# A two-layer MetaFormer with top-2 experts on one Trainium2 core: the second expert bias copied into PSUM, the first experts' weights split earlier, and less work on GpSimd ahead of the routing

## The reference, cut to what matters

```python
x = x + _L0_conv_ref(_ln_c(x), W_qkv, W_proj, b_proj)        # attention over 24 positions, 16 heads
t = _to_tokens(x)
t = t + _L0_ffn_ref(_ln_t(t), gate_w, gate_b, w1, b1, w2, b2)
# layer 0, F = 1024
    for i in range(8):
        h = silu(xf @ w1[i] + b1[i])
        y = h @ w2[i] + b2[i]
        out = out + y * comb[:, i:i + 1]
# layer 1, I = 672
    for e in range(8):
        a, g = split(x @ W1[e] + b1[e], 2)
        out = out + cw[:, e:e + 1] * ((a * silu(g)) @ W2[e] + b2[e])
```

## Time and profile before

| what | value |
|---|---|
| median of three runs | 651.71 us (649.32 to 656.35) |
| the profiled execution's own time | 656.72 us |
| its span, first to last instruction | 655.0 us |
| PE busy | 583.5 us, 89% of the span |
| ACT, DVE, POOL busy | 330.0, 321.6, 291.9 us |
| bias matmuls, line 1342 | 56 |
| layer 0: attention and norms, routing, block loop | about 0 to 80, 80 to 110, 110 to 325 us |
| layer 1: the same | about 325 to 402, 402 to 433, 433 to 655 us |

### The profile page before, as it was taken

How to read it: one execution, slowest core, us unless ns; L and a number is a source line. 1 busy time by engine, 2 the same in 40 slices (tenths; PEclk the granted TensorE clock), 3 DMA queues, 4 the chain that set the end, 5 groups by cost and what they waited for, 6 DMA issues and landing times.

```text
span 655.0 us, 15545 instructions
## 1 busy us (share of the span) xinstructions
PE 583.5 (89%) x3702; PEld 505.7 (77%) x3703; DVE 321.6 (49%) x721; ACT 330.0 (50%) x586; POOL 291.9 (45%) x305
## 2 busy tenths in 40 slices
PE   8997966999999999998879877789999898999982
PEld 4976724888889888987559764279989898999982
DVE  6547583344442445443175386734545454666430
ACT  5683303556554666663157723135656464656430
POOL 3785213355444445544236641324545353555332
PEclk9999678999999999998779987779999898999987
DMA  7425754145432442325122248342254545222120
GB/s 233 132 71 173 241 198 153 25 135 136 125 65 37 125 104 64 69 42 149 21 83 87 85 149 266 131 135 34 38 156 114 160 109 131 74 66 41 36 31 11
DMA packets 43625, 69.35 MB, mean 106 GB/s; under 512 B 5280, under 2 KB 35024, under 8 KB 43600
## 3 DMA queue, kind: packets, MB, share of 16 engines
q1 hardware_dynamic: 32656, 54.86, 26.4%
q0 software_dynamic: 10944, 14.17, 12.1%
HBM read 56.43 MB, written 13.63 MB: 107 GB/s over the span
## 4 chain that ended last, share of the span: by engine, by line
PE 64%; DVE 12%; DMA 12%; issue 5%; ACT 2%; DVEq 2%; ACTq 1%; POOL 1%; POOLq 0%
PE banks L1125 14%; PE banks L1127 13%; PE banks L1126 13%; DMA out_dram<-expert_io,scol 6%; PE banks L1333 5%; PE banks L1156 4%; DMA mid_dram<-expert_io,scol 4%; PE banks L1133 2%; PE banks L1217 2%; DVE stats L830 2%; PE banks L1251 2%; PE banks L1302 2%; DVE onehot_row L1013 2%; PE banks L1240 1%; DVE raw L849 1%
## 5 line engine op out<-in xcount | busy, mean ns | idle before, releaser
L1125 PE MATMUL banks<-w_hi,hT_hi 128*128 (+1 forms) x392 | 120.1, 306 | 14.3 <-DVE hT_lo L1095 14.2
L1125 PE MATMUL banks<-w_hi,xT_hi 128*128 x336 | 121.7, 362 | 3.3 <-DVE xT_lo L1053 2.6
L1127 PE MATMUL banks<-w_hi,xT_lo 128*128 x336 | 116.3, 346 | 0.0
L1126 PE MATMUL banks<-w_lo,xT_hi 128*128 x336 | 115.8, 345 | 0.0
L1127 PE MATMUL banks<-w_hi,hT_lo 128*128 (+1 forms) x392 | 115.2, 294 | 0.0
L1126 PE MATMUL banks<-w_lo,hT_hi 128*128 (+1 forms) x392 | 115.1, 294 | 0.0
L1125 PEld LDWEIGHTS banks<-w_hi,hT_hi 128*128 128x128 f32 (+1 forms) x392 | 78.9, 201 | 21.4 <-issue 20.9
L768 ACT COPY banks<-seed_rows 128x1024 f32 (+1 forms) x58 | 66.7, 1151 | 39.3 <-issue 13.5
L1113 DVE TENSOR_SCALAR expert_io<-banks,gate_tab 128x256 f32<-128x256 f32 x56 | 27.1, 484 | 115.0 <-PE banks L1127 55.3
L599 POOL DMA_INDIRECT mid_dram<-expert_io,scol x28 | 57.6, 2057 | 56.4 <-DVE expert_io L1113 56.4
L561 POOL TENSOR_TENSOR w_lo<-raw,w_hi 128x1024 fp32r<-128x1024 f32 (+1 forms) x24 | 57.2, 2400 | 52.1 <-ACT w_hi L641 51.9
(11 more groups left out here) (188 smaller groups left out, 963.5 us busy)
## 6 DMA issues: line engine op xcount, KB each, us to landing
raw<-in_L_ffn_w_dram SPq DMA_DIRECT2D x32, 512.0 KB, 4.1
raw<-in_L_ffn_W_dram SPq DMA_DIRECT2D x16, 672.0 KB, 4.9
raw<-in_L_ffn_W_dram SPq DMA_DIRECT2D x16, 336.0 KB, 6.1
seed_rows<-in_L_ffn_b_dram SPq DMA_DIRECT2D x8, 672.0 KB, 4.6
seed_rows<-in_L_ffn_b_dram SPq DMA_DIRECT2D x8, 512.0 KB, 4.2
xn_dram<-raw SPq DMA_DIRECT2D x6, 512.0 KB, 3.0
xres<-in_x_dram SPq DMA_DIRECT2D x3, 512.0 KB, 4.5
wqkv<-in_L_conv_W_qkv_dram SPq DMA_DIRECT2D x2, 768.0 KB, 5.9
```

The source lines that it names most:

```text
L1125: pe.matmul(out, hi, w_high, start=first, stop=False, skip_group_check=onto)
L1126: pe.matmul(out, hi, w_low, start=False, stop=False, skip_group_check=onto)
L1127: return pe.matmul(out, lo, w_high, start=False, stop=last, skip_group_check=onto)
```

## The change

1. The bias matmul 1342 goes, and with it `bias_rows`, `expert_sel`, their DMAs, casts, subtractions and selects. SP loads the expert's b2 row, broadcast to 128 partitions, behind its b1 row (two DMAs per expert). ACT copies it to bank 6 in a new `seed_y(b)` at the very end of its `step(b)`, after the weight casts. `seed_y(b)` waits until DVE has read y of block b-1 (`e_sb`), for block 0 until an added fifth `swept` matmul (on bank 6, between PE's step 0 and step 1). PE's second product waits for `y_seeded`. ACT loads two experts from the table in each step instead of one.
2. The first experts' parts are loaded without SP waiting for each; ACT waits for a semaphore of the part (`part_in`). In layer 1 pieces 0 and 1 are cast before the first norm. Piece 3 moves ahead of the exponentials, 4 and 5 into the attention, 8 and 9 take the places between the copies of the product with the values, 10 and 11 come before the square roots of the second norm.
3. POOL makes its second set of constants at the start of the program, and no longer adds `bproj`: DVE does, after the softmax and before its copies of the product with the values.

```diff
             def load_seed(L, e):
-                sp.dma_start(seed_row(L, e % SLOTS), ffn_w[L][3][e].partition_broadcast(P)).then_inc(seed_dma, 16)
+                row, wide = seed_row(L, e % SLOTS), FFN[L].wide
+                sp.dma_start(row[:, 0:wide], ffn_w[L][3][e].partition_broadcast(P)).then_inc(seed_dma, 16)
+                sp.dma_start(row[:, wide:wide + C], ffn_w[L][5][e].partition_broadcast(P)).then_inc(seed_dma, 16)
...
+                    if e < SLOTS:
+                        sp.dma_start(to, src).then_inc(part_in[part], 16)
+                    else:
+                        sp.dma_start(to, src).then_inc(raw_dma[half], 16)
+                        loads[half] += 1
...
-                    if e < SLOTS:
-                        sp.wait_ge(raw_dma[half], 16 * loads[half])
...
-                        act.wait_ge(s.first_in, q + 1)
+                        act.wait_ge(part_in[q % PIECES], 16 * (SLOTS * L + q // PIECES + 1))
...
+                if L == 1:
+                    act.wait_ge(lay[0].moe_done, 1)
+                    first_high(0, 2)
...
                 first_high(2, 3)
                 values_out(2)
+                first_high(3, 4)
                 exponentials(0)
                 exponentials(1)
                 values_out(3)
-                first_high(3, 4)
+                first_high(4, 5)
...
                 attn_out(1)
+                first_high(5, 6)
                 values_out(6)
...
-                first_high(PIECES, PIECES + 2)
+                first_high(6, 8)
...
-                        first_high(PIECES + 2 + j // 2, PIECES + 3 + j // 2)
+                        first_high(8 + j // 2, 9 + j // 2)
...
-                nc.scalar.copy(bias_rows[:, :], bias_raw[:, :]).then_inc(s.bias_cast, 1)
+                first_high(10, 12)
                 nc.scalar.activation(table_out[0:BN, 2 * L:2 * L + 1], row_sum[:, 0:1], ACT.Sqrt)
-                first_high(2 * PIECES, 2 * PIECES + 1)
                 deviations(s.var2, 0, s.std2)
-                first_high(2 * PIECES + 1, 2 * PIECES + 2)
                 deviations(s.var2, 1, s.std2)
-                first_high(2 * PIECES + 2, 2 * PIECES + 3)
...
+                def seed_y(b, e):
+                    if after(b, 1):
+                        act.wait_ge(s.e_sb, b)
+                    else:
+                        act.wait_ge(swept, 5 * (L + 1))
+                    nc.scalar.copy(bank[6][:, 0:C], seed_row(L, e % SLOTS)[:, f.wide:f.wide + C]
+                                   ).then_inc(s.y_seeded, 1)
...
-                    e_next = expert_of(b + 1)
+                    e_here, e_next = expert_of(b), expert_of(b + 1)
                     pieces = piece_range(act, b)
                     xT_high(b + 1)
                     seed(b + 1, e_next)
                     for_pieces(act, pieces, lambda q: split(q, b))
+                    seed_y(b, e_here)
...
+                for g in range(3):
+                    tiles = slice(4 * g, 4 * g + 4)
+                    nc.vector.tensor_tensor(xres[:, tiles, :], xres[:, tiles, :],
+                                            bproj[:, :].unsqueeze(1).to_broadcast([P, 4, C]), ALU.add).then_inc(s.b_added, 1)
                 for j in range(1, 8, 2):
                     dve.wait_ge(s.av_mm, j + 1)
...
-                    if after(b, 1):
-                        pe.wait_ge(s.e_sb, b)
-                    pe.matmul(bank[6][:, 0:C], expert_sel[:, e, :], bias_rows[:, :],
-                              start=True, stop=False)
+                    pe.wait_ge(s.y_seeded, b + 1)
```

More of the change, by code:

```diff
@@ L286, in metaformer @@
         seed_in = sem("seed_in")
+        part_in = [sem(f"part_in{i}") for i in range(PIECES)]
         raw_dma = [sem(f"raw_dma{i}") for i in range(2)]
@@ L409, in load_expert @@
                 kt2 = f.kt // 2
-                for to, src, end in ((w1[:, 0, :], src1[:, 0, :], f.wide), (w1[:, 1, :], src1[:, 1, :], KC * f.wide),
-                                     (w2[:, 0:kt2, :], src2[:, 0:kt2, :], KC * f.wide + kt2 * C),
-                                     (w2[:, kt2:, :], src2[:, kt2:, :], WORDS[L])):
+                parts = ((w1[:, 0, :], src1[:, 0, :], f.wide), (w1[:, 1, :], src1[:, 1, :], KC * f.wide),
+                         (w2[:, 0:kt2, :], src2[:, 0:kt2, :], KC * f.wide + kt2 * C),
+                         (w2[:, kt2:, :], src2[:, kt2:, :], WORDS[L]))
+                for part, (to, src, end) in enumerate(parts):
                     pieces = -(-end // (WORDS[L] // PIECES))
@@ L419, in load_expert @@
                         sp.wait_ge(lay[L].pool_split, PIECES * (e - 1) + pieces)
-                    sp.dma_start(to, src).then_inc(raw_dma[half], 16)
-                    loads[half] += 1
+                    if e < SLOTS:
[3 more added lines that the diff above has]
+                        loads[half] += 1
                     if e >= SLOTS + 2 and pieces == -(-f.wide // (WORDS[L] // PIECES)):
                         seed_loaded(L, e - 2)
-                    if e < SLOTS:
-                        sp.wait_ge(raw_dma[half], 16 * loads[half])
-                        there = end // (WORDS[L] // PIECES)
-                        for _ in range(there - handed[0]):
-                            sp.sem_inc(lay[L].first_in, 1)
-                        handed[0] = there % PIECES
             def expert_loaded(L, half):
@@ L517, in _ @@
             pool.sem_inc(const_done, 1)
+            made(pool.memset(after_or_at[:, :], -1.0))
+            made(pool.affine_select(out=after_or_at[:, :], in_=after_or_at[:, :], compare_op=ALU.is_ge, fill=0.0,
+                                    base=0, pattern=[[-1, P]], channel_multiplier=1))
+            made(pool.memset(ones[:, :], 1.0))
+            made(pool.iota(iota_i[:, :], pattern=[[1, P]], base=0, channel_multiplier=0))
+            made(pool.tensor_copy(iota[:, :], iota_i[:, :]))
@@ L519, in _ @@
+            made(pool.memset(gather_tab[:, TAB:TABLE], 0))
+            made(pool.memset(scan_keep[:, :, :], 1.0))
+            made(pool.memset(scan_keep[:, :, 0:1], 0.0))
+            pool.sem_inc(const_done, 1)
             for L in range(2):
                 s = lay[L]
[L522 to L527 removed]
@@ L747, in _ @@
                 nc.scalar.activation(small[:, 0, :], small[:, 0, :], ACT.Exp).then_inc(s.exp8, 1)
-                act.wait_ge(s.bias_sub, 2)
-                nc.scalar.copy(bias_rows[64:96, :], bias_raw[64:96, :]).then_inc(s.bias_cast, 1)
                 act.wait_ge(s.tab, 2)
@@ L1374, in _ @@
                 pe.wait_ge(s.tab, 3)
+                pe.matmul(bank[6][:, 0:C], busy_in[:, :],
+                          busy_in[:, :].unsqueeze(1).to_broadcast([P, C // P, P]), start=True, stop=True
+                          ).then_inc(swept, 1)
                 step(1)
```

92 lines of the change are left out of this document (21 added, 71 removed).

## The result

The kernel after takes 673.63 us (median of four runs, 669.34 to 674.79), the kernel before beside it 650.78; the ratio on record is 1.0328 (1.0257 to 1.0400); the quotient of the two medians is 1.035. The forecast was 649.3 in a range of 640 to 659. The profiled executions span 671.0 and 655.0 us, 16 apart. The medians are 22.9 apart: the profiled execution of the kernel before was the longest of its four, so the traces show less loss than the medians.

A forecast was written before the change was run, and what follows sets the result against it. PE was taken to bound the kernel, with 64% of the chain. Terms of -11.2 us ahead of the loops, +3.2 for first blocks and +5.6 for the loops gave -2.4, from 651.7 to 649.3 us, range 640 to 659.

The forecast's parts named there:

- b2 broadcasts cost nothing that the chain shows: Loads of the second bias, broadcast to 128 partitions: no cost was counted for them.
- The ring: Block loops: ACT's copy waits for DVE's output, which waits for ACT; 7.1 us per block in layer 0, both loops +5.6.
- longer ring: Rival: ACT's queue from new copy to `xT_hi` takes 0.35 us more per block, loops +15.5, kernel 659.2; chance 0.17.
- Layer 1: Its block loop: 6.8 us per block, PE's pace, but double weight casts and lost catching up after late scatters: +3.8 us.
- The first block: Block 0 of each layer: PE's second product resumes 1.75 us late in layer 0, 1.5 in layer 1; together +3.2.
- The second norm: Ahead of the loops: POOL no longer collides with DVE's normalisation, PE's clock stays up; 6.0 us saved per layer.
- Between the loops: Layer 1 ahead of its loop: norm -6.0, routing -1.6, waits for pieces 8 and 9 +2.4, first block +1.5 us.
- DVE's moved additions: Three `bproj` additions on DVE, about 1.24 us each, 3.7 in a gap of 6.07: no cost.
- the rival of the pieces: Second norm: last pieces stay in the way, one collision and the low clock remain per layer; +4.8, 656.5 us; chance 0.1.
- the port rule: DVE and POOL contend for one port pair, the later blocks fully; three blocked additions cost up to 2.5 us per layer: 654.

The follow-up runs named there:

- after_late: The kernel after with only the second bias's broadcast moved behind the expert's last weight part, with its own semaphore: 661.55 us, 1.0177.
- p23_b2: Parts 2 and 3 on the kernel before, bias matmul kept, plus second-bias broadcasts for experts 3 to 7 into an unread row: 656.96 us, 1.0080.
- p23: The kernel before with parts 2 and 3 of the change alone, bias matmul kept: 645.42 us, 0.9899.
- late89: `p23` with layer 1's splits of pieces 8 and 9 put behind the copies, with 10 and 11: 647.47 us, 0.9951.
- p1: The kernel before with part 1 alone, ACT's copy of the b2 row in place of the bias matmul: 680.9 us, 1.0459.
- moved: The kernel after with the b2 copy taken from the end of ACT's step to behind the next step's `hT_hi` casts: 657.88 us, 1.0089.
- b2late: `moved` with the second bias's broadcast issued whole behind the expert's last weight part, with its own semaphore: 646.43 us, 0.9933.

## Why the prediction was wrong

- **The step that failed outright** is the half sentence that the "b2 broadcasts cost nothing that the chain shows". They cost 12.1 us in the kernel after (25.4 less the 13.3 of `after_late`), 10.6 where the matmul is kept, mostly by making scatters at an expert's change longer: `p23_b2` against `p23`, six of them by 1.0 to 1.6 us. The chain of before already gave DMA 12%, and the late scatters stood there; I had priced the added loads against the queue's mean load and not against the transfer that they fly beside. No rival of the prediction held it. Of the page of the Trainium skill "DMA: Bandwidth & Descriptors", the section "Queues, rings and completion order" says that each DMA engine goes round between the queue rows it has work for and drains a whole packet of one before it turns to the next. Its direction agrees: a load on SyncE's row delays a scatter on GpSimd's. No run shows the packets themselves.
- **The ring was right in kind and mis-sized**: 13.3 us by the loops, 15 to 16 by the medians (below), instead of 5.6. In layer 0 it cost 6.8 instead of 1.8. Round it by the rows above: `xT_hi` start to output end 2.54 in the rows of the chain (forecast 2.53); end of the output 189.17 to the copy 0.18 (0.1); copy to `hT_hi` 0.49 (0.27); `hT_hi` to `xT_hi` 4.01 (4.16). 7.2 instead of 7.06, with most blocks at 7.3. The 0.49 was not thought of: the copy ends the step, so the loop's own branch lies between it and the next instruction. In the chain of the kernel after:

```profile
189.35 0.05 ACT banks L732
189.43 0.05 ACTq L317
189.48 0.19 issue
189.67 0.05 ACTq L317
...
189.84 0.04 ACT hT_hi L751
```

  7.3 is 0.24 more than the forecast 7.06, over 27 blocks 6 us. The rival "longer ring" named branches, though behind the weight cast, and said that it decides from about 0.18 per block. It had 0.17 of the chance. Its price for both loops was 15.5 us, and the ring's measured cost is near that and not near the 5.6 of the forecast; its 659.2 for the kernel is still far from 673.6, because it held the broadcasts at nothing too.
- **Layer 1** had 3.8 for double casts and lost catching up, and `after_late` shows 6.5. Undisturbed blocks are as before (6.7 to 7.2). Behind the late scatters `after_late` has 8.32, 10.84 and 6.50 where before had 7.37, 9.64 and 5.40: 3.25 us from three intervals alone, where I had counted 2.2 for all.
- **The first block**: PE idles 1.90 us in layer 0 (forecast 1.75) and 1.64 in layer 1 (1.5), waiting for `hT_lo` behind the copy; the granted clock was 1.00 in the 6 us behind either.
- **The second norm**: normalisation, clock and route as forecast in both layers, every group at 1.38. The first output came 5.5 us earlier; the forecast was 6.0 less 1.75, so 1.2 more was won. Before, the second group had collided too, 3.42 us in layer 0 and 3.48 in layer 1, and the sum had priced one collision per layer; whether the 1.2 is that one is not shown.
- **Between the loops**: forecast -6.0 - 1.6 + 2.4 + 1.5 = -3.7, measured -3.9. ACT waits 3.29 and 0.70 us for pieces 8 and 9, PE 1.95 for the copy behind, near the 2.4:

```profile
380.50 1.07 ACT L603 CAST w_hi<-raw 128x1056 fp32r<-128x1056 f32 x1 [3.29 <-DMA raw<-in_L_ffn_W_dram]
...
382.20 1.94 PE L1185 MATMUL banks<-raw,region_d 96*96 96x256 f32 x8 [1.95 <-ACT region_a L674]
```

- **DVE's moved additions** took 3.49 us for three, in idle time, from 370.74 on; DVE was not held up. GpSimd's piece subtraction that began beside them was: 4.21 us instead of the 2.43 of the one before it. So the rival of the pieces falls for this kernel, and the port rule held with the roles changed: the additions were first, and the subtraction waited. That was not free. SyncE asks for piece 8's part only when this subtraction, piece 5's, has ended, at 376.54, so about 1.8 of ACT's 3.29 us above came by it (an estimate from 4.21 - 2.43); `p23` shows the same 4.21. `late89` shows the collision on DVE's side, 1.38 us for one group, as soon as the order is changed. It is the exclusive lock of the Trainium skill, "SBUF — State Buffer", "Who interferes with whom", that agrees in both. Timeline of the kernel after, POOL and SyncE's queue:

```profile
367.05 2.43 POOL L529 TENSOR_TENSOR w_lo<-raw,w_hi 128x1056 fp32r<-128x1056 f32 x1 [2.97 <-ACT w_hi L603]
372.30 4.21 POOL L529 TENSOR_TENSOR w_lo<-raw,w_hi 128x1056 fp32r<-128x1056 f32 x1 [2.82 <-ACT w_hi L603]
376.54 2.73 SPq L416 DMA_DIRECT2D raw<-in_L_ffn_W_dram  x2
```

Put together by the traces: -5.5 and -3.9 ahead of the loops, +13.3 ring, +12.1 broadcasts, 16.0. The medians, each less that of before in its job, give the same picture without the long execution of before. Part 1 costs 29.5 (`p1`), parts 2 and 3 win 6.0 (`p23`): 23.5, against the 22.9 measured. The ring is 16.4 (after less `moved`) or 14.7 (`after_late` less `b2late`), the broadcasts' place 12.6 (after less `after_late`) or 10.9 (`moved` less `b2late`), and issuing them there or not at all makes 13.3 (`p23_b2` less `p23`). With both causes removed (`b2late`), no gain of the copy over the matmul shows: its loops sum to 402.7, those of p23 to 400.3. Of the versions with the whole computation p23 has the lowest ratio, 0.9899, and beats both kernels; the intervals of `b2late` (0.9933) and `late89` (0.9951) overlap its own.

## What to carry to other kernels

Before an instruction that waits is put at the end of an engine's step, sum the ring that it closes with the loop's branch and every register load, and ask for an earlier place where the awaited result is already old. Price an added load by the transfer that flies beside it and ends a wait; here the 128 KB loads cost about 13 us at one place in SyncE's queue, and another place gave 11 to 13 of it back. When a wait is removed, look for what its delay kept apart.

## What the runs showed that I had not expected

- The moved broadcast of `b2late` and `after_late` makes one scatter of layer 0 late that had been in time, 7.1 to 7.3 us instead of 5.8: a quiet place for a load is quiet only for the scatters that were late before.
- The 672 KB broadcast of one row to 128 partitions is most of a late scatter's delay in layer 1: 8.12 us with it, 6.21 with one partition of it, beside the same part of 672 KB. No version leaves out the part, so its own share is not shown.
- The loss in the loops is not explained by the granted clock. It was 0.95 and 0.95 in the kernel after, but 0.99 and 0.98 in `after_late`, which keeps the ring, and 0.98 and 0.96 in `p1`, which has the ring and the broadcasts and still shows loops of 421.4 us. Part of the 5.1 us by which after exceeds `p1` there may be clock; it was not separated.
